# Self-attention value products in bursts of four key tiles, with a new order of all engines' work

## The reference

```python
x = attention(ln32(x, ln1), ln32(x, ln1), Wq1, Wkv1, Wo1, bo1) + x     # self, 16 heads of 16
x = attention(ln32(x, ln2), context, Wq2, Wkv2, Wo2, bo2) + x           # cross, 154 keys a sequence
x = geglu_ff(ln32(x, ln3), Wff1, bff1, Wff2, bff2) + x
# the second layer: one head of 256, 154 keys
qp, kp, vp = x @ Wq.T + bq, ctx @ Wk.T + bk, ctx @ Wv.T + bv
out = softmax(qp @ kp.T) @ vp + x
```

## Time and profile before

| what | us |
|---|---|
| median of 3 runs (lowest to highest) | 1716.65 (1714.28 to 1716.99) |
| span of the profiled execution | 1710.7 |
| median less span | 5.95 |
| TensorE busy, share | 1609.0, 94% |
| VectorE busy, share | 1120.2, 65% |
| ScalarE busy, share | 996.5, 58% |
| GpSimd busy, share | 269.4, 16% |
| start of the exponentials of iterations 5, 6, 7, 8 | 95.4, 171.1, 237.0, 310.7 |
| the last exponential of the self-attention ends the iterations at | 1546.9 |

### The profile page before, as it was taken

How to read it: one execution, slowest core, us unless ns; L and a number is a source line. 1 busy time by engine, 2 the same in 40 slices (tenths; PEclk the granted TensorE clock), 3 DMA queues, 4 the chain that set the end, 5 groups by cost and what they waited for, 6 DMA issues and landing times.

```text
span 1710.7 us, 33819 instructions
## 1 busy us (share of the span) xinstructions
PE 1609.0 (94%) x12897; PEld 1019.8 (60%) x12897; DVE 1120.2 (65%) x2221; ACT 996.5 (58%) x2024; POOL 269.4 (16%) x344
## 2 busy tenths in 40 slices
PE   6799999999999999999999999999999999998887
PEld 5444445575756666575756666565656556564666
DVE  4466786867667685867667685867677676824333
ACT  3345767656666666656666666556666566663332
POOL 5201312112102021111102021101010010101100
PEclk9989999999999999999999999999999999997789
DMA  6913241446231231346221231336030321303200
GB/s 175 231 46 121 72 79 58 105 85 136 58 79 46 65 77 51 91 96 136 58 70 41 72 77 42 91 74 135 27 84 23 62 60 38 78 20 76 54 26 13
DMA packets 171647, 129.37 MB, mean 76 GB/s; under 512 B 40751, under 2 KB 161885, under 8 KB 171229
## 3 DMA queue, kind: packets, MB, share of 16 engines
q1 hardware_dynamic: 171421, 127.19, 31.1%
q10 hardware_dynamic: 64, 0.02, 0.0%
HBM read 78.92 MB, written 47.71 MB: 74 GB/s over the span
## 4 chain that ended last, share of the span: by engine, by line
PE 71%; DVE 18%; ACT 5%; issue 3%; DMA 2%; SPq 1%; POOL 0%; DVEq 0%; ACTq 0%; POOLq 0%
PE ps_o L1736 11%; PE ps_max L1702 10%; PE ps_last L1647 9%; PE ps_s L1724 9%; DVE mxh L1373 8%; PE ps_last L1656 6%; PE ps_cross L1615 4%; PE ps_pre L1511 3%; PE ps_pre L1519 3%; DVE mx L1298 3%; PE ps_cross L1601 2%; PE ps_last L1685 2%; DVE th L1330 1%; ACT probs L1152 1%; PE ps_last L1519 1%
## 5 line engine op out<-in xcount | busy, mean ns | idle before, releaser
L1373 DVE TENSOR_REDUCE mxh<-ps_max 128x1 f32<-128x512 f32 x1024 | 659.0, 683 | 221.6 <-PE ps_max L1702 217.7
L1152 ACT ACTIVATE probs<-ps_s 128x512 f32<-128x512 f32 x1024 | 581.1, 597 | 311.7 <-PE ps_s L1724 210.7
L1702 PE MATMUL ps_max<-kst,qst 96*128 96x512 bf16 x1024 | 363.4, 385 | 21.5 <-DVE mxh L1373 15.2
L1724 PE MATMUL ps_s<-qst,kst 98*128 98x256 bf16 x2048 | 371.6, 274 | 6.5 <-ACT probs L1152 4.9
L1736 PE MATMUL ps_o<-probs,vg 128*17 128x256 f32 x4096 | 270.0, 382 | 0.1
L1724 PEld LDWEIGHTS ps_s<-qst,kst 98*128 98x128 bf16 x2048 | 171.7, 98 | 155.7 <-ACT probs L1152 57.9
L1702 PEld LDWEIGHTS ps_max<-kst,qst 96*128 96x128 bf16 x1024 | 94.8, 97 | 143.7 <-DVE mxh L1373 94.0
L1330 DVE SCALAR_TENSOR_TENSOR th<-th,gb 128x256 f32<-128x256 f32 x128 | 66.2, 517 | 151.9 <-ACT gb L1124 151.9
L1736 PEld LDWEIGHTS ps_o<-probs,vg 128*17 128x17 f32 x4096 | 94.1, 96 | 112.2 <-issue 48.3
L1093 ACT ACTIVATE probs<-ps_cross 77x512 f32<-77x512 f32 x224 | 132.4, 591 | 31.7 <-PE ps_cross L1601 30.9
L1647 PE MATMUL ps_last<-y_hi,wff_hi 128*128 128x256 f32 x448 | 140.4, 313 | 10.4 <-DVE hT L1333 7.9
(11 more groups left out here) (265 smaller groups left out, 2016.4 us busy)
## 6 DMA issues: line engine op xcount, KB each, us to landing
parts_s<-qk_parts SPq DMA_DIRECT2D x28, 384.0 KB, 3.8
o_s<-o_sb SPq DMA_DIRECT2D x64, 128.0 KB, 2.8
o_s<-o_sb SPq DMA_DIRECT2D x32, 256.0 KB, 2.2
oT<-o_s SPq DMA_DIRECT2D x62, 128.0 KB
den<-o_s SPq DMA_DIRECT2D x62, 128.0 KB
kst<-parts_s SPq DMA_DIRECT2D x16, 384.0 KB, 5.2
kst<-parts_s SPq DMA_DIRECT2D x48, 128.0 KB, 5.7
qst<-parts_s SPq DMA_DIRECT2D x64, 96.0 KB, 2.7
```

The lines of the kernel that those rows point to most:

```text
L1152: nc.scalar.activation(probs[:, step % PR, 2 * pair:2 * pair + 2, :].rearrange("p j q -> p (j q)"), ps_s[pair][:, :], ACT.Exp, scale=SCALE ...
L1373: nc.vector.tensor_reduce(mxh[:, i // 2, i % 2:i % 2 + 1], ps_max[i % 2][:, :], AX_X, ALU.max).then_inc(g_mx, 1)
L1702: mm(ps_max[i % 2][:, :], qst[0:ROWS, h, q * P:(q + 1) * P], kst[0:ROWS, h, k * 512:(k + 1) * 512], start=True, stop=True).then_inc(g_mt, 1)
L1724: last = mm(ps_s[pair][:, j * CH:(j + 1) * CH], kst[:, h, kt * P:(kt + 1) * P], qst[:, h, :], start=True, stop=True)
```

## The change

A burst V is four key tiles (`VSTEPS` = 4), eight bursts an iteration instead of sixteen. The orders are new: one string for each of the iterations 4 to 7 (`FIRST`, `SECOND`, `THIRD`, `FOURTH`), `STEADY`, `LATE` for 16 to 19, `FINAL` for 20, and `ENDING` for the drain. The setup steps have a letter of their own (s), and counters run through the whole program instead of starting anew in each iteration. The names of the drain's letters differ, its steps stand in the same sequence as before.

```diff
-STEADY = (
-    "lMMMSMcSMSMSMScScSMSMc"
...
+VSTEPS = 4
...
+STEADY = (
+    "McSMSMlSMSMSMpSMSlMSMSMScMcVlcMMScclcMMlSSoSMucSQcSVTSSlccMMlcSS"
...
 def order_of(n):
 
-    return EARLY if n < LAST_LAG else STEADY if n < NCH else LATE
+    if n < LAST_LAG:
+        return (FIRST, SECOND, THIRD, FOURTH)[n - MAX_LAG]
+    return STEADY if n < NCH else LATE if n < END - 1 else FINAL if n < END else ENDING
...
+def chains_of(n):
+
+    if n == END:
+        return dict(m=("mid", NCH - 1), c=("cross", NCH - 2), g=("cross", NCH - 1), l=("last", NCH - 3),
+                    k=("last", NCH - 2), j=("last", NCH - 1))
+    at = dict(p=("pre", n), m=("mid", n - MID_LAG), c=("cross", n - CROSS_LAG), l=("last", n - LAST_LAG))
+    return {letter: (kind, o) for letter, (kind, o) in at.items() if 0 <= o < NCH}
...
+        def walk(n, setup, kinds, work, seen):
+
+            chains = {letter: kinds[kind](o) for letter, (kind, o) in chains_of(n).items()}
             for letter in order_of(n):
-                k = seen[letter]
-                seen[letter] += 1
-                if letter in work:
-                    work[letter](k)
...
+                if letter == "s":
+                    next(setup)
+                elif letter in SHARED:
+                    k = seen[letter]
+                    seen[letter] += 1
+                    if letter in work:
+                        work[letter](k)
                 else:
                     next(chains[letter])
...
-                def values(k):
-                    if not flags[2]:
-                        return
-                    for step in (2 * k, 2 * k + 1):
-                        values_of(SLOTS * (n - ATT_LAG) + step)
+            def values(k):
+                for step in range(VSTEPS * k, VSTEPS * (k + 1)):
+                    values_of(step)
```

More of the change, by code:

```diff
@@ L819, in _ @@
             head()
             setup_work = setup()
-            run(body, range(MAX_LAG, END))
-            store_o(NU - 1)
-            walk_end(mid, cross, last, end_loads)
+            seen = dict.fromkeys(SHARED, 0)
+            run(body)
             sp.wait_ge(c_outst, NCH * 16)
@@ L1398, in _, with body @@
+            def body(n, flags):
+                walk(n, setup_work, dict(pre=pre, mid=lambda o: mid_by(1 - n % 2, n >= LAST_LAG)(o, flags[0]),
+                                         cross=cross_by(not flags[2]), last=last), dict(
+                    M=max_half, Q=max_pairs, T=max_turned, i=lambda o: invert(1, o)), seen)
             head()
             setup_work = setup()
[L1400 to L1402 removed]
@@ L1404, in _ @@
-            run(body, range(MAX_LAG, END))
-            walk_end(mid_by(1 - (END_MID + MID_LAG) % 2, True), cross_by(True), last, end_inverses)
+            seen = dict.fromkeys(SHARED, 0)
+            run(body)
         @block.tensor
@@ new lines, in max_turn, with scores @@
+            def max_turn(unit):
+                pe.wait_ge(g_mp, unit + 1)
+                nc.tensor.transpose(ps_max[0][0:PAIRS, 0:P], mxq[:, :], ident[:, :]).then_inc(g_mT, 1)
+            def scores(k):
+                step, pair = divmod(k, 2)
+                unit, kt = divmod(step, KT)
+                if k == 0:
+                    pe.wait_ge(s_ones, 3)
+                if kt == 0 and pair == 0:
+                    pe.wait_ge(g_shl, (unit + 1) * 32)
+                pe.wait_ge(g_e, max(0, 2 * step + pair - 1))
+                for j in range(2):
+                    h = unit % HG * G + 2 * pair + j
+                    last = mm(ps_s[pair][:, j * CH:(j + 1) * CH], kst[:, h, kt * P:(kt + 1) * P],
+                              qst[:, h, :], start=True, stop=True)
+                last.then_inc(g_s, 1)
@@ new lines, in values_of @@
+            def values_of(step):
+                unit, kt = divmod(step, KT)
+                c, g = divmod(unit, HG)
+                pe.wait_ge(g_e, 2 * step + 2)
+                if kt == 0:
+                    pe.wait_ge(g_v[g], (c // CPB + 1) * 16)
+                    pe.wait_ge(g_o, unit)
+                for j in range(G):
+                    last = mm(ps_o[j * W:j * W + VW, 0:CH], vg[:, g, kt, j * VW:(j + 1) * VW],
+                              probs[:, step % PR, j, :], start=(kt == 0), stop=(kt == KT - 1),
+                              tile_position=(0, j * W))
+                last.then_inc(g_av, 1)
@@ L1750, in _, with body @@
+            def values(k):
+                for step in range(VSTEPS * k, VSTEPS * (k + 1)):
+                    values_of(step)
+            def body(n, flags):
+                walk(n, setup_work, dict(
+                    pre=pre_by(flags[3], flags[4]), mid=lambda o: mid_by(flags[4] and flags[2])(o, flags[0]),
+                    cross=cross_by(not flags[2]), last=last), dict(S=scores, V=values, M=max_scores, T=max_turn), seen)
             head()
             setup_work = setup()
-            run(body, range(MAX_LAG, END))
```

329 lines of the change are left out of this document (111 added, 218 removed).

## The result

The changed kernel takes 1730.6 us (median of 4 runs, 1726.4 to 1733.8), the kernel before 1715.5 beside it. The ratio is 1.0106 with a 95% interval of 1.0077 to 1.0135: it is slower by 1.1%, where 1.7% faster was forecast.

What follows compares the result with a forecast made beforehand. TensorE, busy 94%, was taken to set the pace; steady -16.0, iterations 16 to 19 -5.2, 5 to 7 -5.5 and 20 -2.0 make -28.7 us from 1716.65: 1688 us, 1.7% faster, range 1664 to 1713.

Steps and rivals of the forecast that it cites:

- the border's price: Runs of column-tiled products on TensorE: 0.22 us back per border pair removed, 146 runs, 32.1 us if all counts.
- The 0.33 estimated from the Trainium skill: Other price for a run's border: two tiling-mode drains, 0.33 us a run, 48 us for 146; not used.
- Where VectorE leads: Start of a steady iteration, up to the third burst: VectorE's extra 2.0 us stretches it from 25.1 to 27.1 us.
- The sum: Steady iteration: 27.1 + 66.9 + 0.7 = 94.7 against 96.7 us, so -2.0, eight times: -16.0.
- The ring of four: Bursts reading all four probability buffers wait for the last of eight exponentials: 0.7 us an iteration, the uncertain term.
- the sign of being right: TensorE's waits for the exponential ahead of value bursts: 10 to 40 us in sum.
- the ring eats it up: Rival: bursts needing all four buffers bring 32 us of waits and 24 us of score-pair gaps; 1741 us, chance 0.11.
- Iterations 16 to 19, 20 and the drain: Late part: 92.4 against 93.7 us, -1.3 four times, -5.2; iteration 20 -2.0; drain 0.
- least tight: Iterations 5 to 7, TensorE 4.4 us idle in iteration 6: 25 runs fewer, -5.5 us, other effects taken to cancel.
- the third rival: Relaid order also halves TensorE's 27.5 us idle in iterations 5 to 7 and 16 to 20; 1674 us, chance 0.17.
- The clock: Rival: new waits lower TensorE's clock, 0.05 of iterations 5 to 7, 11 us; 1699 us, chance 0.02.
- the signs of being wrong: Steady iterations of 97 us or more, first stretch well beyond 27, or clock under 1.00 between 200 and 1500 us.

Runs made afterwards that it cites:

- drop_first: old_ring7 with all value products of the first burst of each two left out, borders included; 0.9949 against the kernel before.
- drop_second: old_ring7 with all value products of the second burst of each two left out, borders included; 0.9884 against the kernel before.
- old_half: The kernel before with the value products of every second key tile left out, borders and waits kept; 1690.4 us, 0.9874.
- late_new: The kernel before with the changed kernel's order in iterations 16 to 21 alone; 1704.0 us, 0.9957.
- new_half: The changed kernel with the value products of every second key tile left out, borders and waits kept; 1673.7 us, 0.9768 against the kernel before.
- joined_ring7: old_ring7 with each two bursts joined where the second stood, no other work moved; 1790.2 us, 1.0453 against the kernel before.
- old_ring7: The kernel before with seven probability buffers instead of four, three weights shared and their loads left out; 1713.5 us, 1.0012.
- turn_bare: The kernel before with 26 value bursts moved from directly ahead of a transposing product (turn) to behind it, none joined to another; 1727.5 us, 1.0087.

## Why the prediction was wrong

**The step that failed** is the proviso of the border's price: "each border pair that disappears returns 0.22 us, provided that TensorE is what everybody waits for", and ahead of it "so TensorE sets the pace there", read from 94.65 of 96.9 us busy. The size of the border was right: two short bursts are 2 x 0.99 us and each starts 0.09 us later behind its score pair (0.31 instead of 0.22), a joined one 1.85 and 0.09 once, which is 0.22 less. The 0.33 estimated from the Trainium skill (TensorE: Matmul & The Clock Gate, Single matmul latency, two drains of 166 ns) does not come out here either. The proviso was not right. TensorE was busy because short bursts had been laid into its waits. A full row of busy time did not mean that its products were the path: half of all value products taken away (TensorE 87 us less busy) returned 22 us, at most 7 more having gone to the clock. Joining moves some 0.86 us of products away from the wait that they mostly covered, and saves 0.22. For the eight steady iterations -16.0 us were forecast and +19.6 came.

The Trainium skill has a warning that lies near: Perfetto Trace Analysis, Identifying the Most-Contended Engine, says that matmul busy time doesn't tell how near TensorE is to its roofline, and to judge by the share of weight loads (and by the useful work over the peak). The trace agrees in so far as that share was 60% while the matmul row said 94%. The section speaks of headroom and not of waits with work laid into them; that this work returns little was shown by drop_first, drop_second and old_half.

**Where VectorE leads.** A first stretch of 27.1 us up to the third burst was forecast, and 66.9 behind it. The windows of iteration 13, cut there, columns as the earlier trace rows:

```profile
814.70:843.70 29.00, 27.09 (x246) 16.25 (x249) 26.73 (x58) 17.56 (x34) 3.94 (x7) 1.00 0.38 89
843.70:913.50 69.80, 66.75 (x561) 46.77 (x564) 41.74 (x81) 43.29 (x92) 11.98 (x14) 1.00 0.26 66
```

They took 29.0 and 69.8. VectorE is busy 26.73 us in the first, where the forecast had 25.6 (23.63 + 2.0), and even so not all of the stretch. TensorE is idle 1.9 and 3.05 us in the two where before had 1.1 and 0.9: 2.9 us more, 1.37 of it at the turn without a burst. And it is busy 93.84 us, where before's 94.66 less nine borders (2.0) would be 92.7: 1.2 us more, which I put down to products that stand alone behind a wait. -2.0 + 2.9 + 1.2 is the 2.1 us by which this iteration is longer. The sum had 0.7 for new waits, all of it for the ring. Nothing in it asked what each moved burst had stood in front of.

**The ring of four.** Its price was forecast as 0.7 us an iteration, by a burst that waits for the last of its eight exponentials. It did not show: the burst waits step by step and started 0.31 us behind its score pair, and TensorE was idle 0.0 us ahead of value products, where 10 to 40 us of waits were to be the sign of being right. The waits for exponentials did come, but at the score pairs behind a burst (28.1 us for 4.9), and seven buffers do not remove the loss (1.0097). The rival "the ring eats it up" had the right sign, 1741 us and a wrong reason.

**Iterations 16 to 19, 20 and the drain.** Forecast 92.4, measured 92.2 (iteration 17); against before the four gain 7.3 us, where 5.2 were forecast. Forecast -2.0 for iteration 20, measured -0.9; the drain 163.2 for 163.8 at the same 0.81. The signs held, and late_new shows the gain alone (-0.43%, some -7.4 us). That the sum had -7.2 is partly luck, since its terms were off both ways. Iterations 5 to 7 and the head were forecast at -5.5 and 0 and measured at +5.3 and +5.2. I called them "least tight" and took that as room to gain. Why the late iterations gain and the others do not was not tried; what differs in them is that `pre` has ended, and they have 92 us where the steady ones have 97. The head's +5.2 was not followed up either.

One bound of the range does not follow from its own terms: every saving of the third rival (27.5 us) and no ring wait would end near 1652 us, not at 1664. It bears on nothing here.

**The clock.** The rival gave it 0.02. It did fall, twice, below 1.00 between 200 and 1500 us as the signs of being wrong had it, and took little. Iteration 9 of the changed kernel, TensorE's rows, then the windows of 5 us around them (length, PE busy, granted clock, DMA share, GB/s):

```profile
489.56 1.89 PE L1591 MATMUL ps_last<-wff,hT 128*128 128x256 f32 x8
...
492.82 0.38 PE L1651 MATMUL ps_s<-qst,kst 98*128 98x256 bf16 x2
494.57 0.27 PE L1639 MATMUL ps_max<-ident,mxq 128*8 128x128 f32 x1 [1.37 <-DVE mxq L1325]
494.78 1.06 PE L1550 MATMUL ps_cross<-probs,v 77*17 77x256 f32 x16
495.77 3.68 PE L1446 MATMUL ps_pre<-oT,wq 128*128 128x256 f32 x8
499.24 0.42 PE L1536 MATMUL ps_cross<-q2st,k2st 98*77 98x256 bf16 x2
```
```profile
490.00:495.00 5.00, 3.63 (x25) 1.00 0.09 24
495.00:500.00 5.00, 5.00 (x29) 0.66 0.21 68
500.00:505.00 5.00, 5.00 (x55) 1.00 0.07 27
```

After a wait of 1.37 us at a turn, the eight passes of 495.77 take 3.47 us to the next start, at the 1.2 GHz level; the same shape at 489.56, at the 2.4 GHz level, is 1.89 long instead of 3.68. Iterations 9 and 12 are 1.7 us longer for it, 3.4 of the 21.3 us. The same wait of 1.37 us stands in all eight steady iterations, and the clock fell behind two of them, so the wait alone does not decide it.

## What to carry to other kernels

An engine that is 94% busy isn't thereby the bound: work that can be moved may lie in its waits, and then its duration is nearly free where it stands and costs half to four fifths of itself elsewhere (new_half, drop_first against joined_ring7). Before you price the saving of a merge, look at what stands directly behind each piece in the trace and would have waited without it, or leave the pieces' work out once and see how much of it returns. An order can be judged by stage: here the new one is worth keeping behind iteration 15 alone (late_new, 0.9957).

## What the runs showed of the hardware

Two things I had not expected. An uncovered wait can cost a second time through the clock: in joined_ring7 a wait of 1.64 us for `hT` is followed by the lower level for some 3 us, and a fall like it comes back about once an iteration from 465 us on. Its TensorE row behind the wait, and its windows, columns as above:

```profile
671.15 0.39 PE L1615 MATMUL ps_last<-y_hi,wff_hi 128*128 128x256 f32 x1 [1.64 <-DVE hT L1316]
```
```profile
665.00:670.00 5.00, 4.21 (x27) 1.00 0.02 5
670.00:675.00 5.00, 3.85 (x18) 0.69 0.01 2
```

Over 175 to 1545 us, 23 such windows lie below 1.00; their missing shares come to 22.1 us at full speed, at most that much of the 77 us that joining costs there, while old_ring7 has none. And leaving out work can bring the clock down: drop_first, with 100 us less for TensorE to do, misses 18.7 us in the same way ahead of its drain. The short bursts in the waits seem to have kept the clock up too; that was not tried by itself. turn_bare lost 16 us with no such window at all, with waits of up to 1.4 us, so the clock is an addition to the uncovered waits and not their substance.
